# The loop over the two middle blocks of a DLRM tower, written out as straight code

## The reference

```python
x0 = xk = e                                  # (512, 39, 16), e gathered by ids
for W in (f0, f1, f2):
    z = jnp.einsum('bfd,bgd->bfgd', x0, xk).reshape(b, f * g, d)
    xk = jnp.einsum('bpd,pm->bmd', z, W)     # (512, 128, 16)
    outs.append(xk)
z = jnp.sum(jnp.concatenate(outs, axis=1), axis=-1)
h = jnp.concatenate([z, dense_ctx], axis=1)
h = jnp.maximum(h @ W_top1 + b_top1, 0.0)
h = jnp.maximum(h @ W_top2 + b_top2, 0.0)
y = h @ W_top3
```

## Time and profile before

| | |
|---|---|
| median of 3 runs | 726.46 us (721.77 to 728.2) |
| span of the profiled execution | 726.1 us |
| TensorE, VectorE, ScalarE, GpSimd busy | 686.6, 614.4, 498.4, 255.3 us |
| mean granted clock of TensorE | 0.983 |

### The profile page before, as it was taken

How to read it: one execution, slowest core, us unless ns; L and a number is a source line. 1 busy time by engine, 2 the same in 40 slices (tenths; PEclk the granted TensorE clock), 3 DMA queues, 4 the chain that set the end, 5 groups by cost and what they waited for, 6 DMA issues and landing times.

```text
span 726.1 us, 12749 instructions
## 1 busy us (share of the span) xinstructions
PE 686.6 (95%) x3569; PEld 495.2 (68%) x3569; DVE 614.4 (85%) x1410; ACT 498.4 (69%) x1663; POOL 255.3 (35%) x247
## 2 busy tenths in 40 slices
PE   3769899999999999999999899999999999999998
PEld 0347567667677877766777687766677787777777
DVE  1638899999999866999999676899999986899990
ACT  2136678778786656878786545877878665787882
POOL 5655628137511707126710702415841000111020
PEclk9969999999999999999999989999999999999999
DMA  7181030303020210202111120020303020030000
GB/s 220 10 278 34 7 86 5 90 2 84 14 75 15 49 46 5 76 14 58 41 52 39 25 65 12 22 71 3 94 4 89 1 63 28 1 89 1 0 2 2
DMA packets 23425, 33.99 MB, mean 47 GB/s; under 512 B 7816, under 2 KB 10616, under 8 KB 22967
## 3 DMA queue, kind: packets, MB, share of 16 engines
q1 hardware_dynamic: 18230, 31.84, 14.4%
q0 software_dynamic: 5120, 1.29, 2.0%
HBM read 9.13 MB, written 0.00 MB: 13 GB/s over the span
## 4 chain that ended last, share of the span: by engine, by line
PE 55%; DVE 21%; issue 11%; ACT 2%; DVEq 1%
DVE sums L683 10%; PE x_ps L920 8%; PE v_ps L776 7%; PE v_ps L778 6%; PE v_ps L777 6%; PE a_ps L776 5%; PE a_ps L778 5%; PE a_ps L777 5%; PE s_ps L890 4%; PE s_ps L979 3%; DVE scaled L626 2%; ACT scaled L452 2%; DVE scaled L616 1%; DVE z_sb L656 1%; DVE sums L672 1%
## 5 line engine op out<-in xcount | busy, mean ns | idle before, releaser
L452 ACT ACTIVATE scaled<-a_ps,x0c 128x128 f32<-128x128 f32 x1216 | 350.3, 379 | 144.0 <-PE a_ps L778 135.8
L683 DVE SCALAR_TENSOR_TENSOR sums<-v_ps,x0c,sums 128x128 f32<-128x128 f32 x768 | 214.8, 341 | 38.4 <-PE v_ps L778 38.4
L776 PE MATMUL v_ps<-w_hi,x_hi 128*128 128x512 f32 x320 | 177.8, 556 | 9.1 <-DVE e_parts L574 4.7
L394 POOL DMA_INDIRECT e_sb<-in_tables,ids_now x140 | 165.6, 1183 | 47.3 <-issue 37.3
L410 POOL TENSOR_TENSOR diag_sb<-x0c,eye_sb 128x320 f32<-128x320 f32 x64 | 61.9, 967 | 329.0 <-PE s_ps L979 328.7
L778 PE MATMUL v_ps<-w_hi,x_lo 128*128 128x512 f32 x320 | 127.6, 399 | 0.0
L777 PE MATMUL v_ps<-w_lo,x_hi 128*128 128x512 f32 x320 | 127.5, 398 | 0.0
L776 PE MATMUL a_ps<-w_hi,x_hi 128*128 128x512 f32 (+1 forms) x320 | 124.5, 389 | 0.0
L777 PE MATMUL a_ps<-w_lo,x_hi 128*128 128x512 f32 (+1 forms) x320 | 123.7, 387 | 0.0
L778 PE MATMUL a_ps<-w_hi,x_lo 128*128 128x512 f32 (+1 forms) x320 | 123.5, 386 | 0.0
L920 PE MATMUL x_ps<-z_sb,w_sb 117*128 117x512 f32 (+1 forms) x210 | 109.5, 602 | 5.9 <-DVE z_sb L656 5.8
(11 more groups left out here) (110 smaller groups left out, 644.9 us busy)
## 6 DMA issues: line engine op xcount, KB each, us to landing
b_sb<-a_sb SPq DMA_DIRECT2D x300, 78.0 KB
w_sb<-in_w SPq DMA_DIRECT2D x1, 2496.0 KB
e_sb<-in_tables,ids_now POOLq DMA_INDIRECT x140
s_sb<-in_w SPq DMA_DIRECT2D x2, 1024.0 KB, 5.3
wt_sb<-in_wt SPq DMA_DIRECT2D x1, 768.0 KB
s_sb<-in_w SPq DMA_DIRECT2D x1, 512.0 KB, 10.5
wt_sb<-in_wt SPq DMA_DIRECT2D x1, 512.0 KB
w_raw<-in_w0a SPq DMA_DIRECT2D x1, 409.5 KB
```

The lines of the kernel that those rows point to most:

```text
L394: pool.indirect_dma_start(out=e_sb[0:rows, i, :], out_offset=None, in_=tables, in_offset=bass.IndirectOffsetOnAxis(ap=ids_now[0:rows, 0, i ...
L452: last = nc.scalar.activation(scaled[:, s % 2, to, j, :], bank[:, j * MAPS:(j + 1) * MAPS], ACT.Copy, scale=x0c[:, k % 4, s, lo + j:lo + j ...
L683: nc.vector.scalar_tensor_tensor(out=sums[:, s % 2, j, :], in0=v_ps[n % 2][:, j * MAPS:(j + 1) * MAPS], scalar=x0c[:, k % 4, s, lo + j:lo ...
L776: nc.tensor.matmul(to, high, w_high, start=True, stop=False)
```

## The change

The register loop over blocks 1 and 2 is replaced by a loop at the time the program is written, so that all four blocks are issued with t as a number. Slot (0, 0) stays ahead of it; the order of the slots is the same as before. Nothing else is changed.

```diff
             one(0, -1)
-            for k in range(PER_BT + 1):
-                one(0, k)
-            with eng.Fori(1, B // BT - 1) as t:
+            one(0, 0)
+            for t in range(B // BT):
                 for k in range(1, PER_BT + 1):
                     one(t, k)
-            for k in range(1, PER_BT + 1):
-                one(B // BT - 1, k)
             one(B // BT, 1)
```

## The result

The straight kernel takes 721.16 us (median of 11 runs, 718.88 to 723.37) against 727.37 us (11 runs, 721.77 to 729.39) for the kernel before. The ratio is 0.9921, 95% interval 0.9902 to 0.9939: 0.8% less, where 1.1% was forecast. The time lies within the range.

A forecast was written before the change was run, and what follows sets the result against it. TensorE, busy 95% of a 726.1 us span, held 55% of the chain, VectorE 21%. Jump 5.85 plus counting 2.3 is 8.15 us off, a span of 717.9; 0.4 more gives 718.3 us, 1.1% less, range 713.5 to 724.5.

The forecast's parts named there:

- The 108 ns: Skill's figure for a compare-and-branch, by which removing one jump saves next to nothing; the prediction set the traced 5.20 us against it.
- The jump, 5.85 us: Between chunks 8 and 9: TensorE's pause at the loop's jump back and the low clock after it go, saving 5.85 us.
- The net figure: Jump's price from stages: chunk 8 against 12, 3.85 us, plus chunk 9 against 5, 2.00 us; sum 5.85 us.
- the gross one: Jump's price before any catching up: TensorE's idle time of 3.3 us and 2.9 us lost to low clock, together 6.2.
- The counting, 2.3 us: Register instructions before waits in blocks 1 and 2 go: 1.15 us a pass, 2.3 us for both, bounds 0 and 3.
- The pair at k = 4: Chunk 12 in the loop against straight chunk 4: 43.30 - 42.85 = 0.45 us, put down to counting in registers.
- The note that chunk 13 lacks the gathers: Chunk 13 lacks GpSimd's gathers issued beside chunk 5, so some of the 0.35 us counted at k = 1 may stay.
- What comes: Straight code needs its own instruction pages; nothing taken for it, but a late page would cost 5.85 us.
- The slower rival, late pages: Straight code's instruction pages reach TensorE late; from two on slower than before (730.0 us), three 735.9; several late pages chance 0.04.
- The median of the runs is 0.4 above the span: Step from span to time: median 726.46 us against profiled span 726.1, so a span of 717.9 gives 718.3 us.
- only the pause goes: Rival: the jump's 5.85 us goes but counting is not saved, giving 720.6 us, within 1%; chance 0.20.
- about 1%: What a measurement of this kernel can tell from no change, with a time known to some 3 us either way.

The follow-up runs named there:

- the short jump: Straight kernel with a two-pass loop over one already met wait, on every engine, between blocks 1 and 2: 721.34 us, ratio 0.9929 to the kernel before.
- the kernel with registers and no jump: Against the kernel before, blocks 1 and 2 written out on all engines, with t still from a register set by hand: 721.99 us, ratio 0.9933.
- the hinted loop: Kernel before with a prefetch hint for the jump's target at the head of the loop's body on every engine: 725.28 us, ratio 0.9990.
- in the second: Unchanged copies of both kernels, run again: kernel before 726.03 us, straight kernel 720.98 us, ratio 0.9944 (0.9925 to 0.9964).
- VectorE's loop: Against the kernel before, only VectorE keeps the loop and all other engines are straight: 721.90 us, ratio 0.9945.

## Why the prediction was right, and where its sizes were off

**The mechanism** is shown. The jump back over a block makes TensorE fetch the loop's head: the taken branch costs 5.14 to 5.30 us in three traces of the kernel before, 0.23 over a few instructions, 0.25 with the code asked for in advance. By the Trainium skill, page "Runtime: NRT & Kernel Launch", section "Instruction fetch mechanics", a taken branch to code outside the small window held by the engine forces a fetch before it goes on; the traces agree. The 108 ns of the Trainium skill's page "Advanced Engine Details and Errata", section "Control Flow Timing", weighed in the prediction, lies between what the branch not taken (0.08 us) and the short jump (0.23 us) cost on TensorE, and says nothing of a far one.

**The jump, 5.85 us.** Measured 6.24 us in the first trace, by the kernel with registers and no jump, 6.3 and 5.0 in the other two (blocks 1 and 2 take 341.91 and 340.62 us there, against 335.60). The term is right for the traced execution, which had the full price of the clock; it is not a constant, for the clock's part in chunk 9 goes from 0.7 to 2.2 us in the three traces. The net figure came out 0.4 us small because chunk 8 was laid beside chunk 12, which is longer by its place: without a jump chunk 8 takes 42.94 us, not 43.30. With that the net price is the gross one, the 6.2 us of pause and slow matmuls, and in that trace nothing of it was caught up. In the runs without a trace the same spread shows: of 18 runs of the kernel before made beside the last experiments, five had a mean granted clock of 0.991 and took 722.9 to 723.5 us, seven had 0.986 and took 725.8 to 727.6. That the first five had no low clock after the pause is argued from this, not shown.

**The counting, 2.3 us.** Measured 1.4 to 1.7 us, 335.60 less the 333.9 to 334.2 us of three straight traces. The pair at k = 4 was misread: chunk 12 is longer than chunk 4 in straight code too (43.63 to 42.85), and it did not fall by 0.2 to 0.4 us but rose by 0.3, for a reason that stays open. So the sum, 8.15 for the 7.90 traced, came so near in part by luck: the one misread pair made the jump too small and the counting too large. The note that chunk 13 lacks the gathers and part of k = 1 may stay was needless: with gathers beside it chunk 5 fell to 47.21, and chunk 9 to 47.20.

**What comes** cost nothing in straight code: no gap on issue of 1 us before a matmul of TensorE or an operation of VectorE in chunks 5 to 15, in any of the three traces. The slower rival, late pages, was no fancy though: the hinted loop met what I take for one, 1.7 us on VectorE.

**From the trace to the median.** This is the step that was off. "The median of the runs is 0.4 above the span" took one execution's span and another's time for a pair. The straight kernel's own list has both for one execution: 718.88 us and a span of 717.1, 1.8 apart, and 1.8 to 2.3 in the traced runs of all experiments. So the traced execution of the kernel before took some 727.9 us by estimate (726.1 + 1.8; the 728.2 of its list fits), above the 726.46 I started from, and the sum of 8.15 off it gives 719.8. The rest, to the median of 721.16, is argued and not shown: the traced executions were a long one before and, after, the shortest of 11, and the median run of each kernel has its own share of low clock. The jump's price was not always paid in full before, and the end costs 1.6 us in some runs after (one of three traces of the straight kernel, and those of the short jump, of the hinted loop and of VectorE's loop). Against 7.9 us in the traced blocks the ratios leave 4.4 to 7.1 us in the first measurement and 2.6 to 5.4 in the second. How often each happens, and whether the drop at the end is more frequent where the pause at the jump is missing, stays open: the drop stands in four of the nine traces without an idle TensorE at the jump and in none of the five with one, too few to tell.

**The chances.** A gain of over 1% had 0.52 and a change within 1% had 0.44; the 0.8% measured is the second. The median, 721.16, is nearer to "only the pause goes" (720.6) than to the forecast (718.3), but that rival is wrong: by the stages the counting went too, so that its time is near proves nothing for it. Half of it is so: in place of the register instructions more semaphore instructions stand in VectorE's straight code (555 records, 325 before), but they cost less. Two sentences of the prediction on its own certainty were off. An interval of 0.6 to 1.0% is clear of no change, so "about 1%" took the scatter of single runs for that of a median; and the lower end of the range does not follow from its terms, for 718.3 less 0.7 of counting and 3 of scatter is 714.6, not 713.5.

## What to carry to other kernels

The loop here was cheap inside (1.4 to 1.7 us in some 340) and dear at its jump back (5.0 to 6.3 us). To find such a price, cut the span at the same instruction of each pass and look at the pass boundary: the jump over a large body showed there as idle time that nothing releases and, after the pauses of 3.3 to 3.4 us, as a low clock. Before writing the loop out, try a prefetch hint on the engine that is the bound: here it brought most of the gain in one instruction. Look at the code after the loop as well, where VectorE stood 1.7 us once it had the hint too. And size a gain of 1% from several traces of both kernels, with the span and the time of the same execution.

## What the runs showed that was not expected

- Jumps of several engines at one time cost more than the sum: TensorE's taken branch took 3.58 us with its own loop alone and 4.86 with VectorE's (one trace each), and 5.14 to 5.30 with all five.
- A pause of VectorE of 2.3 us costs 0.8, since TensorE is the bound of the stage; one of 1.6 on TensorE costs 1.7.
- A pause of 3.0 us on TensorE was followed by the full clock in one kernel (chunk 9 in 47.52 us at 1.00), one of 3.3 to 3.4 by the low one in the kernel before (0.95, 0.95 and 0.98).
- The hint on VectorE took the pause at the jump away and brought one of 1.7 us some 50 us after the loop had ended (one trace).
